# A two-layer graph and expert network: the first bias moved into the cleared banks, one weight loaded first, and a shorter list of late slots

## The reference, cut to what matters

```python
x = x + L0_gnn(layernorm(x))   # agg = segment_sum(features[src] * edge_weight, dst); agg @ W.T + b
x = x + L0_ffn(layernorm(x))   # the top half of the nodes by a router go through gelu(x @ w1 + b1) @ w2 + b2
x = x + L1_gnn(layernorm(x))   # 16 relations: (h @ weight[r]) gated by a sigmoid, gathered by edge, summed, relu
x = x + L1_ffn(layernorm(x))   # 8 experts, the best two per node
```

## Time and profile before

| | us |
|---|---|
| median of 3 runs (3487.45 to 3488.27) | 3487.49 |
| the profiled execution | 3485.95 |
| its span, first to last instruction | 3484.1 |
| prelude, up to the first gather | 0 to 99.5 |
| first gather, issues of GpSimd | 100.2 to 1093 |
| `Choose` | 1125 to 1171 |
| second gather, issues of GpSimd | 1720 to 2724 |
| experts | 2811 to 3484 |

### The profile page before, as it was taken

One profiled execution on the slowest core, in us unless ns is written; L12 is line 12 of the kernel. 1 busy time (PEld: TensorE's weight loads), 2 busy tenths in 40 slices (PEclk: granted clock), 3 DMA queues, 4 the chain that ended last, 5 costly groups with the idle time before them and its releaser, 6 DMA issues. The chain is left out here.

```text
span 3484.1 us, 60502 instructions
## 1 busy us (share of the span) xinstructions
PE 2641.0 (76%) x14275; PEld 1945.1 (56%) x14276; DVE 1735.5 (50%) x5654; ACT 722.1 (21%) x1906; POOL 1907.2 (55%) x1974
## 2 busy tenths in 40 slices
PE   7588888887885599999755556565555379999997
PEld 6477777776764344444344444444444257777675
DVE  6455555554552645555355555444544455455454
ACT  4121211111110133333201000000000143333332
POOL 4777777777774000000177777777777235555554
PEclk9799999999998799999888888777777579999998
DMA  6333333333332244444455544555454432322232
GB/s 210 96 112 111 112 112 113 113 113 112 113 110 62 97 199 199 195 196 197 183 152 151 148 147 151 153 150 150 146 147 146 175 107 44 49 47 45 46 48 34
DMA packets 175344, 434.54 MB, mean 125 GB/s; under 512 B 41728, under 2 KB 103808, under 8 KB 168864
## 3 DMA queue, kind: packets, MB, share of 16 engines
q0 software_dynamic: 97264, 236.73, 26.3%
q1 hardware_dynamic: 56576, 183.45, 13.8%
q10 hardware_dynamic: 21424, 13.57, 1.3%
HBM read 275.57 MB, written 158.04 MB: 124 GB/s over the span
## 5 line engine op out<-in xcount | busy, mean ns | idle before, releaser
L756 POOL DMA_INDIRECT g_msg<-table,idx x1568 | 1518.9, 969 | 477.8 <-issue 477.8
L826 PE MATMUL psum<-g_msg,g_hot 128*128 x3328 | 989.3, 465 | 604.9 <-SPq L704 387.2
L826 PEld LDWEIGHTS psum<-g_msg,g_hot 128*128 128x128 f32 x3328 | 773.2, 238 | 806.2 <-issue 663.5
L776 DVE TENSOR_SCALAR g_hot<-iota,g_cols 128x128 f32<-128x128 f32 x1664 | 451.4, 365 | 31.7 <-DVE g_cols L773 29.3
L750 POOL MEMSET g_zeros<- 128x256 f32 x2 | 0.6, 311 | 628.6 <-POOLq L1331 627.5
L1834 POOL DMA_INDIRECT out<-ex_y,ex_to x112 | 203.4, 1816 | 246.1 <-DMA out<-ex_y,ex_to 166.0
L1533 PE MATMUL psum<-wrel_halves,t_xhi 128*128 128x512 f16 x784 | 297.7, 380 | 1.8 <-DVE t_row L1431 1.8
L1535 PE MATMUL psum<-wrel_halves,t_xlo 128*128 128x512 f16 x784 | 297.6, 380 | 0.0
L1534 PE MATMUL psum<-wrel_halves,t_xhi 128*128 128x512 f16 x784 | 297.6, 380 | 0.0
L1431 DVE TENSOR_SCALAR t_row<-psum,t_gate 128x256 f32<-128x256 f32 x392 | 171.4, 479 | 238.8 <-PE psum L1535 237.3
L1986 PE MATMUL psum<-w,ex_ghi 128*128 x784 | 259.6, 381 | 7.0 <-DVE ex_y L1897 6.4
(11 more groups left out here) (351 smaller groups left out, 3278.9 us busy)
## 6 DMA issues: line engine op xcount, KB each, us to landing
table<-t_row SPq DMA_DIRECT2D x49, 2048.0 KB, 6.3
g_msg<-table,idx POOLq DMA_INDIRECT x1568
piece_stage<-in_w SPq DMA_DIRECT2D x32, 512.0 KB, 5.7
w_halves<-piece_halves SPq DMA_DIRECT2D x32, 512.0 KB, 3.4
w<-w_halves SPq DMA_DIRECT2D x8, 2048.0 KB, 22.5
rows<-sc_row ACTq DMA_DIRECT2D x50, 128.0 KB, 2.1
out<-acc ACTq DMA_DIRECT2D x49, 128.0 KB
table<-t_row SPq DMA_DIRECT2D x24, 256.0 KB, 2.4
```

The costliest lines, as they stand in the source:

```text
L756: pool.indirect_dma_start(out=msg[:, at:at + D], out_offset=None, in_=table, in_offset=bass.IndirectOffsetOnAxis(ap=t[f"idx{g}"][:, n:n + ...
L776: last = nc.vector.tensor_scalar(hot[b][:, k * P:(k + 1) * P], t["iota32"][:, :], c3[:, k, where:where + 1], c3[:, k, weight:weight + 1], ...
L826: pe.matmul(ps, hot[b % PAIR][:, k * P:(k + 1) * P], msg[:, bass.ds(slot_at[k], D)], start=False, stop=False, skip_group_check=True).then_ ...
```

## The change

Three edits.

1. The bias. GpSimd's 50 additions in the prelude are gone, and its waits ahead of them. The first gather gets `base`, the tile of the bias in all partitions, in the place of `zeros`: ScalarE writes it into the banks where it wrote zeros, at the start and after each window. Ahead of that TensorE writes it into the four banks by one product each with the identity. GpSimd clears a tile of zeros for the second gather alone.
2. The identity and `w0` are loaded by SyncE, ahead of `x`, instead of by ScalarE.
3. The late part: two slots are written out, and behind them one branch on the first entry of `late` goes around a loop over six groups of eight. `late` has six entries, and there are 102 slots in all instead of 108.

```diff
+LATE_FIRST = 2
+LATE_REST = -(-(WINDOWS + LAG - LATE_FIRST) // GROUP_SLOTS) * GROUP_SLOTS
+LATE = LATE_FIRST + LATE_REST
@@ prelude, SyncE
+            sp.dma_start(t["ident"][:, :], dram["ident"]).then_inc(w0_loaded, 16)
+            sp.dma_start(w0[:, :]..., dram["w0T"]...).then_inc(w0_loaded, 16)
             for k, (a, b) in enumerate(zip(X_CUTS, X_CUTS[1:])):
                 sp.dma_start(acc[:, a:b, :], ...)
@@ prelude, ScalarE
-            act.dma_start(t["ident"][:, :], dram["ident"]).then_inc(w0_loaded, 16)
-            act.dma_start(w0[:, :]..., dram["w0T"]...).then_inc(w0_loaded, 16)
             act.dma_start(last[:, :], ...)
@@ prelude, GpSimd
-            pool.wait_ge(ready, 5)
-            pool.wait_ge(consts_loaded, 16 * 10)
-            for n in range(TILES):
-                pool.wait_ge(turn_done, min(n + 1, WINDOWS))
-                nc.gpsimd.tensor_tensor(tile_of(t["acc"], n), tile_of(t["acc"], n), t["b0"][:, :], ALU.add).then_inc(bias_done, 1)
-            pool.wait_ge(bias_done, TILES + 1)
+            pool.wait_ge(side_clear, 1)
@@ gather
-    zeros = w.sb(f"{name}_zeros", [P, D], F32)
+    origin = base or w.sb(f"{name}_origin", [P, D], F32)
     def late(eng, step, tiles=False):
-        with eng.Fori(0, LATE // GROUP_SLOTS) as i:
-            any_ = eng.value_load(t["late"][0:1, bass.ds(i, 1)], min_val=0, max_val=GROUP_SLOTS)
-            with eng.If(any_ >= 1):
-                with eng.Fori(0, GROUP_SLOTS) as k:
-                    slots(eng, step, TURNS + i * GROUP_SLOTS + k, tiles)
+        for k in range(LATE_FIRST):
+            slots(eng, step, TURNS + k, tiles)
+        more = eng.value_load(t["late"][0:1, 0:1], min_val=0, max_val=GROUP_SLOTS)
+        with eng.If(more >= 1):
+            with eng.Fori(0, LATE_REST // GROUP_SLOTS) as i:
+                any_ = eng.value_load(t["late"][0:1, bass.ds(i, 1)], min_val=0, max_val=GROUP_SLOTS)
+                with eng.If(any_ >= 1):
+                    with eng.Fori(0, GROUP_SLOTS) as k:
+                        slots(eng, step, TURNS + LATE_FIRST + i * GROUP_SLOTS + k, tiles)
@@ gather, GpSimd
-            pool.memset(zeros[:, :], 0.0).then_inc(zeroed, 1)
+            if not base:
+                pool.memset(origin[:, :], 0.0).then_inc(zeroed, 1)
@@ gather, TensorE, ahead of follow.tensor_first(pe)
+            for b in range(BANKS if base else 0):
+                pe.matmul(core.bank[b][:, 0:D], t["ident"][:, :], base[:, :], start=True, stop=True).then_inc(zeroed, 1)
@@ gather, ScalarE: clear(b) and close(n) copy origin in the place of zeros
-            act.wait_ge(zeroed, 1)
+            act.wait_ge(zeroed, BANKS if base else 1)
@@ program
-        gather(core, t, dram["table0"], 0, t["side"], after, pieces, depth, chosen)
+        gather(core, t, dram["table0"], 0, t["side"], after, pieces, depth, chosen, base=t["b0"])
```

More of the change, by code:

```diff
@@ L74 @@
 GROUP_SLOTS = 8
-LATE = -(-(WINDOWS + LAG) // GROUP_SLOTS) * GROUP_SLOTS
+LATE_FIRST = 2
+LATE_REST = -(-(WINDOWS + LAG - LATE_FIRST) // GROUP_SLOTS) * GROUP_SLOTS
+LATE = LATE_FIRST + LATE_REST
 TURNS = NB // 2
@@ L249, in prelude @@
     ones_made, summed, centred, counted, rooted = core.sems("ones_made", "w0_summed", "w0_centred", "t0_counted", "t0_rooted")
-    turn_done, xT_done, mm_done, row_done, bias_done = core.sems(
-        "t0_turn_done", "t0_xT_done", "t0_mm_done", "t0_row_done", "t0_bias_done")
+    turn_done, xT_done, mm_done, row_done, side_clear = core.sems(
+        "t0_turn_done", "t0_xT_done", "t0_mm_done", "t0_row_done", "t0_side_clear")
     stored = [core.sem(f"t0_stored{c}") for c in range(ROWS_AHEAD)]
@@ L273, in _ @@
             acc = t["acc"][:, :].rearrange("p (n d) -> p n d", d=D)
+            sp.dma_start(t["ident"][:, :], dram["ident"]).then_inc(w0_loaded, 16)
+            sp.dma_start(w0[:, :].rearrange("p (c o) -> p c o", c=KC), dram["w0T"].rearrange("(c p) o -> p c o", p=P)).then_inc(w0_loaded, 16)
             for k, (a, b) in enumerate(zip(X_CUTS, X_CUTS[1:])):
@@ L356, in _ @@
                       allow_small_or_imprecise_dtypes=True).then_inc(iotad, 1)
-            pool.memset(t["side"][:, WINDOWS * D:], 0.0).then_inc(bias_done, 1)
+            pool.memset(t["side"][:, WINDOWS * D:], 0.0).then_inc(side_clear, 1)
             pool.wait_ge(steps_known, 1)
@@ L505, in _ @@
                 chain(nc.vector.tensor_copy(slot[:, :, column], prior[:, :]))
-            chain(nc.vector.tensor_tensor(count[0:1, 0:LATE // GROUP_SLOTS], count[0:1, TURNS + GROUP_SLOTS - 1:SLOTS:GROUP_SLOTS],
-                                          count[0:1, TURNS - 1:SLOTS - GROUP_SLOTS:GROUP_SLOTS], ALU.subtract))
-            chain(nc.vector.tensor_copy(t["late"][:, :], count[0:1, 0:LATE // GROUP_SLOTS]))
+            chain(nc.vector.tensor_tensor(count[0:1, 0:LATE_REST // GROUP_SLOTS], count[0:1, SLOTS - LATE_REST + GROUP_SLOTS - 1:SLOTS:GROUP_SLOTS],
+                                          count[0:1, SLOTS - LATE_REST - 1:SLOTS - GROUP_SLOTS:GROUP_SLOTS], ALU.subtract))
+            chain(nc.vector.tensor_copy(t["late"][:, :], count[0:1, 0:LATE_REST // GROUP_SLOTS]))
             chain(nc.vector.tensor_copy(code[:, :, BATCH:BATCH + BATCH // BANKS], wins[0:1, 0:NB, BANKS - 1:BATCH:BANKS]))
@@ L651, in halve, with gather @@
         self.nc.vector.scalar_tensor_tensor(out=lo, in0=stage, scalar=W_SCALE, in1=hi, op0=ALU.mult, op1=ALU.subtract).then_inc(self.lo_done, 1)
-def gather(core, t, table, g, out, weights, pieces, follow, then=None):
+def gather(core, t, table, g, out, weights, pieces, follow, then=None, base=None):
     nc = core.nc
@@ L840, in clear @@
             def clear(b):
-                nc.scalar.activation(core.bank[b][:, 0:D], zeros[:, :], ACT.Copy).then_inc(bank_free, 1)
+                nc.scalar.activation(core.bank[b][:, 0:D], origin[:, :], ACT.Copy).then_inc(bank_free, 1)
             def close(n):
@@ L850, in close @@
                 core.hold(act, "act", copied, n + 1)
-                nc.scalar.activation(ps, zeros[:, :], ACT.Copy).then_inc(bank_free, 1)
+                nc.scalar.activation(ps, origin[:, :], ACT.Copy).then_inc(bank_free, 1)
             def close_from(k, m, start, end):
@@ L2037, in program @@
             ("idx1", [P, EDGE_ROWS], I32), ("step_cols", [P, STEP_COLS * COLS], F32), ("code", [1, NB * CODE], I32), ("freed", [1, TILE_BATCHES], I32),
-            ("last_step", [1, WINDOWS], I32), ("closed", [1, NB + 1], I32), ("slot", [1, SLOTS * SLOT], I32), ("late", [1, LATE // GROUP_SLOTS], I32),
+            ("last_step", [1, WINDOWS], I32), ("closed", [1, NB + 1], I32), ("slot", [1, SLOTS * SLOT], I32), ("late", [1, LATE_REST // GROUP_SLOTS], I32),
         ):
```

1 line of the change is left out of this document (removed).

## The result

| | before | after |
|---|---|---|
| median | 3487.47 us (3483.83 to 3488.27, 4 runs) | 3435.61 us (3431.56 to 3437.69, 4 runs) |
| ratio | | 0.9855, interval 0.9844 to 0.9867 |
| profiled execution | 3485.95, span 3484.1 | 3437.13, span 3435.2 |

A forecast was written before the change was run, and what follows sets the result against it. GpSimd's 1568 gather issues, 1.273 us per gather issue pair, were taken to bound both gathers, so gains at the seams add: prelude 20.5, first late part 17.0, second 14.5, together 52.0 us, forecasting 3435.5 us, range 3429 to 3444.

The forecast's parts named there:

- D: Rival: gather issues begin 20.5 us sooner, but landings or the ring hold them later; 3456 us, chance 0.04.
- E: Rival: the pace of GpSimd's gather issues gets worse, 33 ns per issue cancelling the gain; chance 0.03.
- F: Rival: more than two windows have late slots, so the late parts give nothing; 3467 us, chance 0.02.
- The additions: Prelude's end: without GpSimd's 50 additions SyncE is the last to arrive, 18.5 us gained.
- The zero tile: Ahead of the first gather issue: dropping the clearing gains between 0 and 0.69 us, taken as 0.5.
- The start: Prelude's start: with SyncE loading identity and `w0` ahead of `x`, TensorE's first turn comes at 6.7, 1.5 us gained.
- The first walk: First gather's late part: VectorE's 16.66 us pause over empty slots and groups shrinks, 14.5 us gained.
- the other bound: Late part: the remaining empty slot and branch, written out, cost 0.6 to 0.9 us each, so 15.2 us go.
- the gelu: End of the first gather: a candidate for what is late next, claimed to move with the late part.
- The clock: Behind the first late part: TensorE stays at 2.4 GHz, down product 3.62 instead of 6.18 us, 2.5 us gained.
- The second walk: Second gather's late part: TensorE's 16.74 us pause shrinks, 14.5 us gained, no clock gain.
- Rival B: Late parts: jumps stop for an instruction fetch at 2.4 us, 5 to 10 us less gain, 3440 to 3445; chance 0.10.

The follow-up runs named there:

- `bias_adds`: Changed kernel with the 50 GpSimd additions and zeros in the banks put back, late part and loads as changed: 3459.56 us, 0.9908 of the kernel before.
- `again`: The changed kernel run once more without edit: 3436.84 us, 0.9845 of the kernel before; repeated on another chip (`again_b`): 4075.04 us, 0.9864.
- `loads_act`: Changed kernel with the identity and `w0` loaded by ScalarE again: 3436.20 us, 0.9838 of the kernel before.
- `best`: Changed kernel with one late slot written out, identity and `w0` loaded by ScalarE, half the experts' weights held until the facts' store landed: 4036.37 us, 0.9881 of kernel before.
- `late_one_facts`: Changed kernel with one late slot written out and half the experts' weights held until the facts' store landed: 4067.90 us, 0.9857 of the kernel before.
- `late_old_warm`: Changed kernel with the old late part, TensorE doing unused products during the first gather's walk: 4056.49 us, 0.9945 of the kernel before; repeated: 4099.90 us, 0.9938.
- `facts_first`: Changed kernel, SyncE holding half the experts' weights until the facts' store landed: 4028.99 us, 0.9875 of the kernel before; repeated: 4067.86 us, 0.9870.
- `after`: The changed kernel without further edit, in its first profiled execution: 3437.13 us.
- sets 2 and 3: The second and third of three sets of experiment runs, each with the kernel before beside it, which took 4083.04 and 4127.45 us there against 3490.99 in the first.

## Why the prediction was right, point by point

- **The bound.** GpSimd's pace did not move (969 ns, 477.4 us of "issue"), and the first seam's 19.8 us were still 19.7 at the gather's end. Rivals D and E fell, and so did F: with more than two late slots the pauses would have stayed.
- **The additions, 18.5 us forecast.** GpSimd's place at the block's end was taken by SyncE, as said. The pair of profiles gives 19.8 for the whole seam and `bias_adds` against `again` 19.5. What is over 18.5 in the pair is the wait for the last store, 1.1 us instead of 3.1, less the later first turn; in `again` it is mostly the first turn, 1.0 us earlier than before. Both differ by execution.
- **The zero tile, 0.5 us: nothing.** GpSimd was released at 99.4 and issued at 100.17; now it is released at 79.6 and issues at 80.40, 0.8 us behind it both times (0.8 in `bias_adds` too). The clearing lay in the lead that the first issue has in any case: my lower bound.
- **The start, 1.5 us: wrong, the step that failed.** I took `x`'s 4.94 us from issue to landing as its own, and let it be merely issued a microsecond later. With the identity and `w0` ahead in the same queue it took 7.3 (5.4 in `again`, issued at 1.65 and landed at 7.09). TensorE needs all three tiles, and the last to land was `x` in every execution with SyncE's loads, `w0` in every one with ScalarE's. The forecast turn at 6.7 was reached by the earliest of 11. Measured: -0.9 us in the pair of profiles, +0.8 on average over 14 executions, and nothing that the time can show. The Trainium skill, "DMA: Bandwidth & Descriptors", section "Issuing engines are not separate DMA queues", says that loads issued by different engines share the same DMA engines, and that issuing from several saves only the sequencer's time; that agrees with `loads_act`, whose time is the same to 0.6 us.
- **The first walk, 14.5 us.** Measured 15.1 (16.66 - 1.52) on VectorE and 15.0 on TensorE. Written out, a load and a branch cost less than the 1.22 and 1.36 us of a step in a loop: `best` and `late_one_facts` split the 1.52 into 0.55 for the empty slot and 0.97 for the branch, so the other bound, 0.6 to 0.9 each, was right in the sum. I had named the gelu as what could be late next and let it move with the late part. It doesn't: it starts 0.3 us behind the slot's last product, before (1109.43) as after (1089.76), and it is what the down product now waits for.
- **The clock, 2.5 us.** Measured 2.5 in the product; VectorE's two waits give 2.3. `late_old_warm` isolates it (2.2 to 2.5). But three of ten executions with a short pause fell to the lower level all the same, so it is a gain of some 2.5 in most executions and 0.8 in some (6.18 - 5.41).
- **The second walk, 14.5 us.** 15.7 at TensorE (16.74 - 1.00), 15.3 between the rows.
- **The seam at `Place`: 0 forecast, 0.9 to 1.5 given back.** The store of the facts was the hidden second wait; `facts_first` shows it.
- **The experts.** 2.6 us longer in this pair; they are 673.5 to 679.2 over all executions, and the mean store of line 1838 took 1816 to 1869 ns. The forecast had 2 to 3 us of either sign for a gather's pace and none for the experts; their spread is not explained. The pair of profiles gives 48.9 us and the medians 51.9, since the profiled execution before lies 1.5 us under its median and the one after 1.5 over it. The errors, of both signs (0.9 at `Place`, 2.4 at the start, 0.5 for the zero tile and 2.6 in the experts, against 0.6 and 0.8 in the walks and 2 in the last store's landing), are of the size of the spread between executions. That the forecast hit to 0.1 us is luck: parts of it were off by up to 2.6 us, the pair of profiles is 3.1 short of it, and the medians happen to make that good.
- **Rival B.** No stop at the jumps: pauses of 1.52 and 1.02 us leave no room for 2.4. Blocks of instructions are moved there, though: in the DMA view of `after` one of 8 KB between 1089.8 and 1090.0 and one of 16 KB between 1090.2 and 1090.4, the first of them 1.2 us into VectorE's pause of 1.52. In all eight executions with two slots the first starts 0.3 us ahead of VectorE's next instruction and ends behind that instruction's start, so VectorE did not wait for it. By the rule of the Trainium skill cited in the prediction ("Runtime: NRT & Kernel Launch", "Instruction fetch mechanics"), a far target would first have to be fetched; either the targets were held or the fetch was done in time, and no run here shows which, nor for which engine these blocks were.

## What to carry to other kernels

Look for the gain at the seams where all engines meet: what an engine does there beyond the second-latest is the whole of the gain, and taking away what stands out gave nearly all of it here (18.2 us of 19.5 for 26 of 50 additions). Next to each seam write down the *second* wait and the third with their distance, above all small stores behind large loads; where the next wait is on another engine, as the gelu was here, a shorter pause gives nothing more. Steps of a loop that a table leaves empty cost over a microsecond each on the engine that everything waits for, and let TensorE's clock fall for the first product behind them. A term of a microsecond that rests on when one load landed is not to be taken from one profile; here the same program had 2 us of spread.

## What the runs showed of the hardware that was not expected

The sets 2 and 3 ran on other chips, where the kernel before took 17 to 18% longer. The GpSimd issues are as long as ever (946 ns, the median), but GpSimd now waits for places of the ring. Waits of GpSimd in `again_b`:

```profile
POOL g_msg L758 <- SPq L711: 663.3, 97, 14.0
...
POOL g_msg L758 <- issue: 449.3, 1470, 0.5
```

SyncE frees no places because TensorE is late, and TensorE is late without waiting for anything that the profile shows. Line 1048 (the up products) of `again`, then of `again_b`; each has 1600 records:

```profile
L1048 PE MATMUL psum<-f_xT,w 128*128 128x128 f32 x1600 | 186.8, 275 | 0.0
```
```profile
L1048 PE MATMUL psum<-f_xT,w 128*128 128x128 f32 x1600 | 286.0, 319 | 342.5 <-issue 341.8
```

And the timeline of TensorE in `again_b`, inside one run of 32 such products:

```profile
627.14 1.61 PE L1048 MATMUL psum<-f_xT,w 128*128 128x128 f32 x13
630.54 0.27 PE L1048 MATMUL psum<-f_xT,w 128*128 128x128 f32 x1 [1.78 <-issue]
...
635.49 0.37 PE L1048 MATMUL psum<-f_xT,w 128*128 128x128 f32 x1 [2.44 <-issue]
```

258 such pauses of up to 3.2 us stand ahead of that line, which runs in the first gather alone, in the middle of products whose inputs are there; on the first chip there is none. Ahead of line 830, in both gathers, such time is 337.5 us, in `again` 152.1. The issues of the first gather take 1466 us (991 in `again`), those of the second 1161 (1000). What TensorE waits for there no view shows, and it stays open. It is hardly its instructions as the DMA view has them: the queues of instructions move 16 blocks between 100 and 1500 us, far fewer than the pauses. For the change it mattered little: the gain was 52.4 us there too. Whether the chips themselves or their state at the time made the difference isn't shown. For the method it matters that a program's bound can be another one on another chip, so that versions are compared only within one set of runs.
